# A decoder's mixtures of experts: a first tile per expert at a fixed place, gates fetched with the tokens and applied as the result leaves PSUM, outputs scattered to their tokens and added by column

## What is computed

```python
_, selected = jax.lax.top_k(scores + expert_bias[None, :], K)
top_scores = jnp.take_along_axis(scores, selected, axis=1)
top_scores = top_scores / (top_scores.sum(-1, keepdims=True) + 1e-20)
shared = jax.nn.silu(x @ shared_gate_w) * (x @ shared_up_w) @ shared_down_w
comb = jnp.zeros((T, E), jnp.float32).at[jnp.arange(T)[:, None], selected].add(top_scores)
for e in range(E):
    gu = x @ experts_gate_up[e]
    g, u = jnp.split(gu, 2, axis=-1)
    routed = routed + comb[:, e:e + 1] * (jax.nn.silu(g) * u @ experts_down[e])
return (shared + routed).reshape(b, s, h)
```

## Time and profile before

| | |
|---|---|
| median of 3 runs | 3533.64 us (3531.35 to 3537.07) |
| profiled execution, own time | 3534.41 us |
| its span, first to last instruction | 3532.6 us |
| TensorE busy | 3000.9 us (85%) |
| VectorE, ScalarE, GpSimd busy | 1560.5, 1036.7, 469.2 us |
| mean granted TensorE clock | 0.914 of full speed |
| moved by DMA | 319.04 MB, mean 90 GB/s |

### The profile page before, as it was taken

How to read it: one execution, slowest core, us unless ns; L and a number is a source line. 1 busy time by engine, 2 the same in 40 slices (tenths; PEclk the granted TensorE clock), 3 DMA queues, 4 the chain that set the end, 5 groups by cost and what they waited for, 6 DMA issues and landing times.

```text
span 3532.6 us, 36213 instructions
## 1 busy us (share of the span) xinstructions
PE 3000.9 (85%) x14276; PEld 1880.4 (53%) x14276; DVE 1560.5 (44%) x2609; ACT 1036.7 (29%) x2982; POOL 469.2 (13%) x494
## 2 busy tenths in 40 slices
PE   7889989998889999789598989999787877999951
PEld 4445454554655565467354555555444455777740
DVE  5510277103835555410365656566365667000026
ACT  3210161101723333212172223223135441444420
POOL 0000000000000000022201212120010001555555
PEclk9889989999899999899798999999798867999985
DMA  3011102100011110179300010011000002999964
GB/s 149 17 44 42 60 15 70 43 29 1 17 36 45 43 47 30 48 283 326 95 24 11 31 45 32 19 39 36 24 18 22 1 1 77 368 361 366 364 216 116
DMA packets 78377, 319.04 MB, mean 90 GB/s; under 512 B 13408, under 2 KB 13408, under 8 KB 66432
## 3 DMA queue, kind: packets, MB, share of 16 engines
q0 software_dynamic: 39264, 186.30, 15.0%
q1 hardware_dynamic: 16880, 90.19, 7.2%
q10 hardware_dynamic: 22064, 40.25, 3.1%
HBM read 274.80 MB, written 41.88 MB: 90 GB/s over the span
## 4 chain that ended last, share of the span: by engine, by line
PE 71%; DVE 17%; ACT 7%; issue 3%; POOL 2%; DMA 1%; POOLq 0%; ACTq 0%; SPq 0%; DVEq 0%
PE P L878 32%; PE P L880 14%; PE P L1199 9%; PE P L1097 3%; PE P L1079 3%; ACT A L1314 3%; PE P L886 3%; DVE A L1475 2%; PE P L891 2%; DVE A L1916 1%; POOL A L2000 1%; DVE A L1727 1%; DVE A L1725 1%; DVE A L1726 1%; ACT A L1431 1%
## 5 line engine op out<-in xcount | busy, mean ns | idle before, releaser
L878 PE MATMUL P<-A,W 128*128 128x400 f32 (+1 forms) x1888 | 691.4, 506 | 10.3 <-DVE A L1755 6.8
L1246 ACT ACTIVATE A<-P 128x400 f32<-128x400 f32 (+5 forms) x770 | 411.8, 543 | 969.1 <-PE P L880 452.3
L878 PEld LDWEIGHTS P<-A,W 128*128 128x128 f32 x1888 | 362.5, 195 | 283.9 <-issue 33.7
L2000 POOL DMA_INDIRECT A<-experts,A x141 | 134.3, 952 | 2010.2 <-DVE A L1901 1855.3
L886 PE MATMUL P<-C,A 128*128 128x128 f32 (+4 forms) x1553 | 230.4, 273 | 163.1 <-DVE A L1925 130.6
L878 PE MATMUL P<-X,W 128*128 128x400 f32 x864 | 336.6, 528 | 34.4 <-DVE X L1579 30.1
L1199 PEld LDWEIGHTS P<-A 128*128 128x128 f32 x2704 | 328.6, 194 | 69.2 <-issue 41.0
L1199 PE MATMUL P<-A 128*128 128x128 f32 x2704 | 329.6, 277 | 1.4 <-ACT A L1246 1.4
L886 PEld LDWEIGHTS P<-C,A 128*128 128x128 f32 (+4 forms) x1553 | 181.8, 149 | 206.1 <-DVE A L1925 140.1
L1916 DVE TENSOR_TENSOR A<-P,A 128x128 f32<-128x128 f32 (+1 forms) x141 | 44.9, 318 | 552.9 <-ACT A L1431 552.9
L878 PEld LDWEIGHTS P<-X,W 128*128 128x128 f32 x864 | 170.1, 201 | 165.6 <-DVE X L1579 34.1
(11 more groups left out here) (230 smaller groups left out, 3746.1 us busy)
## 6 DMA issues: line engine op xcount, KB each, us to landing
W<-weights SPq DMA_DIRECT2D x60, 1024.0 KB, 4.8
slot_outputs<-A ACTq DMA_DIRECT2D x141, 256.0 KB
W<-weights SPq DMA_DIRECT2D x32, 448.0 KB, 3.4
x_by_token<-A ACTq DMA_DIRECT2D x16, 200.0 KB
A<-experts,A POOLq DMA_INDIRECT x141
A<-x_by_token,A POOLq DMA_INDIRECT x141
W<-weights SPq DMA_DIRECT2D x8, 256.0 KB, 2.6
C<-constants SPq DMA_DIRECT2D x1, 1990.5 KB, 17.2
```

The lines of the kernel that those rows point to most:

```text
L878: self.e.matmul(out, a, b, start=i == 0, stop=False)
L1246: self.e.activation(out, in_, ACT.Copy).then_inc(*self.of(*item))
L2000: self.e.indirect_dma_start(out, None, table, bass.IndirectOffsetOnAxis(ap=idx, axis=0)).then_inc(sem, 16)
```

## The change

Places of tokens. Each expert now owns one tile of its own (`NT` = experts + `NO`), and what it has beyond 128 tokens goes into `NO` further tiles (12 and 49); the totals stay 28 and 113. Since an own tile's expert is known when the program is built, its weights are loaded by plain DMAs from SyncE (`experts`); only the further tiles' weights are fetched by an indirect DMA. `c.seq` is the order of tiles: some own tiles, then own and further ones in turn, own ones at the end. Indirect DMAs carry a bound, and rows whose index lies beyond it (empty slots, unused tiles) are not moved. Weights have 3 places in sublayer 5 and 9 in sublayer 11, of which seven are outside the old ones (dead key buffers, ring slots).

Gates. The 16 or 64 gates of a token are stored behind its 512 features (`gates_out`), come with the token rows, are picked by VectorE (`gate`), and ScalarE applies them as the scale of the copy out of PSUM. The result goes by an indirect scatter (`give`, GpSimd) to row token*kk+j of `outputs`.

Pipeline. `stages` is now fetch, two idle, xturn, up, one idle, down, give: at step t, give of tile t-7, down of t-6, up of t-4, turn of t-3, fetch of t, in both sublayers.

Adding up. `collect` is gone. SyncE loads the results of choice j for four batches at once (`YJ`, 100x4x512), two for each j, from the last j down, and VectorE adds them whole (`column`): 4 in sublayer 5, 16 in sublayer 11. In sublayer 11 the first 10 stand between the last steps of the pipeline.

Lists. `lists` is cut into `ranks`, `places`, `by_token`, `listed` and `indices`, laced with the shared expert's steps; `shared_down` comes behind them all. One of the two one-hot matrices is made by GpSimd (`place_hot`), the other by VectorE (`tile_hot`). The loops that picked gates per choice are gone. The output is stored in two halves.

```diff
-GATHERS, STORES = 16, 4
+GATHERS, STORES = 10, 9
...
-        c.NT = (T * kk + 127 * E) // 128
+        c.NO = (T * kk - kk) // 128
+        c.NT = E + c.NO
...
+        stored = [("x_stored", n, b) for b in range(NB)]
+        if n == 5:
+            c.YJ = [self.ar(3072 + 2048 * i, 4, 512) for i in range(2)]
+            c.R = 3
+            c.places = lambda: [(self.ar(12096, 3072), stored), (self.ar(21280, 3072), [("proj", "sdown", n, NB - 1)]),
+                                (self.ar(0, 3072), [("choice", n, "gates")])]
+        else:
+            c.YJ = [self.ar(2048 * i, 4, 512) for i in range(3)]
+            c.R = 9
+            idle = [("x", 7, 1)]
+            c.places = lambda: [(self.KF[:, 0:1536], idle), (self.KT[:, 0:1536], idle), (self.KT[:, 1536:3072], idle)] + [
+                (self.ring[:, SLOT * (i % RING):SLOT * (i % RING) + 1536], [self.loads[i].free]) for i in self.before(pre, "up")] + [
+                (self.ar(12096, 1536), stored), (self.ar(13632, 1536), stored)]
+        R = c.R
+        c.seq, o = [], 0
+        for e in range(E):
+            c.seq.append((c.NO + e, e))
+            while o < c.NO and e < E - kk and (o + 1) * (E - kk - R) <= (e + 1 - R) * c.NO:
+                c.seq.append((o, None))
+                o += 1
+        assert o == c.NO and all(e is not None for _, e in c.seq[:R]) and all(e is not None for _, e in c.seq[-kk:])
...
-        for f in range(c.nf):
-            for h in range(2):
-                yield "shared", c, f, h
+        both = [(f, h) for f in range(c.nf) for h in range(2)]
+        yield "ranks", c
+        for f, h in both[:2]:
+            yield "shared", c, f, h
+        yield "places", c
+        yield "shared_glu", c, 0, 0
+        yield "by_token", c
+        yield "shared_glu", c, 0, 1
+        for f, h in both[2:]:
+            yield "shared", c, f, h
+        yield "weigh_choice", c
+        for f, h in both[2:]:
+            yield "shared_glu", c, f, h
+        yield "gates_out", c
+        yield "listed", c
+        yield "indices", c
         for b in range(NB):
             yield "shared_down", c, b
-        yield "lists", c
-        idle = 2 if c.nf == 1 else 0
-        stages = ["fetch"] + [None] * idle + ["xturn", "up", "down"]
+        stages = ["fetch", None, None, "xturn", "up", None, "down", "give"]
+        columns = [("column", c, u) for u in range(2 * c.kk)]
+        landed = c.NT - c.kk + len(stages) + 1 + (c.n == 11)
         for t in range(c.NT + len(stages) - 1):
             for i in range(len(stages) - 1, -1, -1):
                 if stages[i] and 0 <= t - i < c.NT:
                     yield stages[i], c, t - i
-        first = [("norm_add", c, 0), ("norm_centre", c, 0), ("norm_scale", c, 0)]
+            if t >= landed:
+                yield columns.pop(0)
+                yield columns.pop(0)
+        yield from columns
+        first, tail = ([s for s in steps if s] for steps in self.norms(c))
         for b in range(NB):
-            for j in range(c.kk):
-                yield "collect", c, b, j
             yield "combine", c, b
             if b in (3, 4, 5):
                 yield first.pop(0)
-        return [("norm_add", c, 1), ("norm_centre", c, 1), ("norm_scale", c, 1)]
+        return tail
...
     def down(self, c, i):
         self.wait_ge(self.at("proj", "edown", c.n, i))
-        if i >= 3:
-            self.wait_ge(self.at("y_stored", c.n, i - 3))
-        self.copy(c.Y[:, i % 3, :], self.ps("proj", "edown", c.n, i)[:, :], "y", c.n, i)
-        self.wait_ge(self.at("y", c.n, i))
-        self.store(c.YD[128 * i:128 * i + 128, :], c.Y[:, i % 3, :], "y_stored", c.n, i)
+        ny = c.Y.shape[1]
+        if i >= ny:
+            self.wait_ge(self.at("given", c.n, i - ny))
+        self.wait_ge(self.at("gate", c.n, i))
+        self.e.activation(c.Y[:, i % ny, :], self.ps("proj", "edown", c.n, i)[:, :], ACT.Copy,
+                          scale=c.GW[:, i % 8:i % 8 + 1]).then_inc(*self.of("y", c.n, i))
 
...
+    def listed(self, c):
+        n, kk, NT = c.n, c.kk, c.NT
+        mark, after = self.marks(c)
+        after("tile_f")
+        for i in range(NB * kk):
+            b, j = i // kk, i % kk
+            if i >= 6:
+                self.wait_ge(self.at("plan", "list", n, i - 6))
+            self.e.tensor_scalar(c.OA[0:S, i % 6, 0:NT], self.c["tiles"][0:S, 0:NT], c.FT[0:S, b, j:j + 1],
+                                 c.DV[0:S, b, j:j + 1], ALU.is_equal, ALU.mult).then_inc(*self.of("tile_hot", n, i))
...
+    def column(self, c, u):
+
+        h = u % 2
+        a = c.ACC[0:S, 4 * h:4 * h + 4, :]
+        for part in range(2):
+            self.wait_ge(self.at("got_y", c.n, u, part))
+        if u < 2:
+            for b in range(4 * h, 4 * h + 4):
+                self.wait_ge(self.at("acc", c.n, b, -1))
+        else:
+            self.wait_ge(self.at("col", c.n, u - 2))
+        self.e.tensor_tensor(a, a, c.YJ[u % len(c.YJ)][0:S], ALU.add).then_inc(*self.of("col", c.n, u))
 
     def combine(self, c, b):
         self.wait_ge(self.at("turn", "acc", c.n, b))
...
+    def listed(self, c):
+
+        self.wait_ge(self.at("place_f", c.n))
+        for b in range(NB):
+            if b >= 4:
+                self.wait_ge(self.at("plan", "list", c.n, c.kk * (b - 3) - 1))
+            for j in range(c.kk):
+                i = self.e.tensor_scalar(c.OB[0:S, b % 4, j, :], self.c["slots"][0:S, :], c.FP[0:S, b, j:j + 1], None, ALU.is_equal)
+            i.then_inc(*self.of("place_hot", c.n, b))
+
     def fetch(self, c, i):
-        n = c.n
+        n, (d, expert) = c.n, c.seq[i]
         if i == 0:
             self.wait_ge(self.at("rows", n))
-            self.wait_ge(self.at("token_of", n))
+            self.wait_ge(self.at("indices", n))
+            self.wait_ge(self.at("empty_x", n))
             for b in range(NB):
                 self.wait_ge(self.at("x_stored", n, b))
-        if i == c.late:
-            self.wait_ge(self.at("listing", n, ("gate", c.kk - 1)))
-        if i >= len(c.WT):
-            self.wait_ge(self.at("proj", "edown", n, i - len(c.WT)))
-        self.gather(c.WT[i % len(c.WT)], c.table, c.WI[:, i:i + 1], "got_w", n, i)
-        if i == 0:
-            self.wait_ge(self.at("proj", "sdown", n, NB - 1))
-            self.wait_ge(self.at("acc", n, NB - 1, -1))
+            self.wait_ge(self.at("gates_stored", n))
+        if expert is None:
+            self.wait_ge(self.at("proj", "edown", n, i - c.R))
+            self.rows(c.places()[i % c.R][0], None, c.table, c.WI[:, d:d + 1], 128 * c.E - 1, "got_w", n, i)
         if i >= 4:
             self.wait_ge(self.at("turn", "x", n, i - 4))
-        self.gather(c.XG[:, i % 4, :], self.k.XD[:, :], c.TI[:, i:i + 1], "got_x", n, i)
-
-    def collect(self, c, b, j):
-        m = b * c.kk + j
-        if m == 0:
-            for i in range(c.NT - STORES, c.NT):
-                self.wait_ge(self.at("y_stored", c.n, i))
-            self.wait_ge(self.at("proj", "edown", c.n, c.NT - 1))
-        if m >= 8:
-            self.wait_ge(self.at("acc", c.n, (m - 8) // c.kk, (m - 8) % c.kk))
-        self.gather(c.YG[0:S, m % 8, :], c.YD[:, :], c.SI[0:S, b, j:j + 1], "got_y", c.n, m)
+            self.wait_ge(self.at("gate", n, i - 4))
+        self.rows(c.XG[:, i % 4, :], None, c.XD[:, :], c.TI[:, d:d + 1], T - 1, "got_x", n, i)
+
+    def give(self, c, i):
+        d = c.seq[i][0]
+        self.wait_ge(self.at("y", c.n, i))
+        self.rows(c.YD[:, :], c.YI[:, d:d + 1], c.Y[:, i % c.Y.shape[1], :], None, T * c.kk - 1, "given", c.n, i)
...
+    def experts(self, c):
+
+
+        R = c.R
+        for i, (d, expert) in enumerate(c.seq):
+            if expert is None:
+                continue
+            place, needs = c.places()[i % R]
+            for item in needs if i < R else [("proj", "edown", c.n, i - R)]:
+                self.wait_ge(self.at(*item))
+            self.dma(f"expert{i % R}", place, c.table[128 * expert:128 * expert + 128, :], "got_w", c.n, i)
+        by_column = c.YD.rearrange("(b s j) n -> j s b n", b=NB, j=c.kk)
+        given = 0
+        for u in range(2 * c.kk):
+            j, h = c.kk - 1 - u // 2, u % 2
+            for i in range(given, c.NT - j):
+                self.wait_ge(self.at("given", c.n, i))
+            given = c.NT - j
+            if u >= len(c.YJ):
+                self.wait_ge(self.at("col", c.n, u - len(c.YJ)))
+            for part, rows in enumerate((slice(0, 96), slice(96, S))):
+                self.dma(f"given{u % 3}_{part}", c.YJ[u % len(c.YJ)][rows], by_column[j, rows, 4 * h:4 * h + 4, :], "got_y", c.n, u, part)
...
+            if p.index >= RING and k.loads[p.index - RING].name == ("L2_attn_", "qk", 1):
+                self.experts(k.subs[5])
+            self.piece(p, wd)
+        self.experts(k.subs[11])
```

More of the change, by code:

```diff
@@ L1853, in lists, with places @@
+    def places(self, c):
+        E, n, sm = c.E, c.n, self.k.small
+        mark, after = self.marks(c)
```

(11 more changed lines are left out.)

273 lines of the change are left out of this document (157 added, 116 removed).

## The result

The changed kernel takes 3498.05 us (median of 4 runs, 3491.65 to 3499.11) against 3532.67 (4 runs, 3531.35 to 3537.07): a ratio of 0.9895, 95% interval 0.9883 to 0.9908. It is faster by 1%. The prediction said 3429 and 3398 to 3466: right in direction, but 69 us too low, and the measured time lies above the range. The profiled execution is the quickest of the four, with an own time of 3491.65 and a span of 3489.8.

A forecast was written before the change was run, and what follows sets the result against it. TensorE and its hand-offs were taken to pace sublayer 11's loop, DMA only just keeping up. 3532.6 - 23 - 31 - 56 + 5 (sublayer 5) = 3427.6 us span, forecast 3429 us, 8-in-10 range 3398 to 3466.

The forecast's parts named there:

- skipped rows cost like moved ones: Rival for both tile loops: unmoved rows cost full DMA time, +37 and +13 us, giving 3479; chance 7%.
- GpSimd sets the loop: Rival for sublayer 11's loop: indirect DMAs at 1.454 us make GpSimd set the pace, +27 us, giving 3456; chance 14%.
- the clock in sublayer 5: Rival: each stall lowers TensorE's clock for a tile, 1.5 to 2 us nine times, giving 3445; chance 10%.
- Sublayer 11's start, -23 forecast: Sublayer 11 before its tile loop: one-hots shared by two engines, gate loops gone, first `down` at 2975 against 2998.
- end at 2960.5: Sublayer 11's lists: one-hots start at 2940 and end at 2960.5, GpSimd taking 0.3 us each; 0.45 would add 9.
- The rival of one-hots in turns: Sublayer 11's lists: VectorE and GpSimd block each other, their one-hot times add up, +10 us, giving 3439; chance 12%.
- Sublayer 5's loop, +27 forecast: Sublayer 5's tile loop: three weight places cause stalls costing +45 us, shorter steps of 5.83 us give back 18.
- a wait of under 1 us that the following stall swallows: Sublayer 5's loop: own tiles' weights land in 6.0 plus 0.5 us against steps of 5.83, at no net cost.
- Sublayer 5's start, -9 forecast: Sublayer 5 before its loop: expert loads wait for `shared_down`, ending 1495.5; first `down` at 1516 against 1525.5.
- The ends, -56 and -12 forecast: Behind the last `down`: column loads and adds replace gathers, 71.4 against 127.6 us in sublayer 11, 35.7 against 48.1 in 5.
- loads of 800 KB land in 4.25 us: Column loads at the ends: with three places and 2.33 us of adding, 2.3 us a column, just hidden.
- Sublayer 11's loop, -31 forecast: Sublayer 11's tile loop: 112 steps of 3.36 us, 376 against 407; at 3.18, hand-off fully hidden, -51.

The follow-up runs named there:

- e1: Changed kernel with both one-hot matrices of the lists made by VectorE, none by GpSimd: 3571.0 us, sublayer 11's start 79.6 us.
- e5: Changed kernel with four places of weights in sublayer 5 instead of three, long pipeline kept: 3425.1 us, ratio 0.9691 to the kernel before.
- f1: Changed kernel with VectorE one-hots, four weight places in sublayer 5, its first own weights queued ahead of the dense pieces, columns read in one stretch: 3401.6 us.
- f2 to f4: Three single edits of the changed kernel: most adding left out; columns read in one unbroken stretch; expert weights read instead of results. 3490.0, 3492.7, 3498.0 us.
- g2: Changed kernel with result columns in unbroken 800 KB stretches, each loaded into 128 partitions of 1600 elements instead of 96 and 4 of 2048: 3474.1 us.
- h1: Changed kernel with unbroken result columns, loads writing only partitions 0 to 63 and almost no adding: 3566.7 us, sublayer 11's end 73.2 us.
- h2: Changed kernel with unbroken result columns, loads writing only partitions 32 to 95 and almost no adding: 3540.0 us, sublayer 11's end 61.9 us.
- f2: Changed kernel with VectorE adding only 8 of 512 features of each column, loads, places and waits as they were: 3490.0 us.
- c1_after_again: The changed kernel itself run once more, unedited, on a second chip: 3494.5 us, ratio 0.9888 to the kernel before.

## Why the prediction failed

Of the 69 us, 62 are in the profiled execution, and the stages below add up to them; the rest is that the median lies 6.4 us above that execution, where the sum had it 0.8 under. Five stages missed by 8 to 19 us each, and one came out 9 us better. The two rivals nearest to 3498, 3479 (skipped rows cost like moved ones) and 3456 (GpSimd sets the loop), are near by luck: in sublayer 11's loop the DMA share is 0.60 and TensorE has no wait in the step shown. What did come of the rivals is the clock in sublayer 5.

**Sublayer 11's start, -23 forecast, -4.0 measured.** The step that failed is "end at 2960.5: GpSimd is the slower hand, and I give it 0.3 us each, as VectorE's 0.29", with a price of 0.45 as the worse case. GpSimd takes 0.59 to 0.69 each, 64 of them 40.0 us where 20.5 were counted. The one-hots did begin where the sum had them, even 7 us sooner (29.7 us behind the router's second half, which is 2933 in before's trace). Another 6.4 us lie between the last one-hot and the first `down`: 4.3 until `shared_down` starts, since TensorE can work off the last batch of eight pairs only then, and 9.9 us for `shared_down` in one row where 7.7 were counted. A price taken from another engine's row is no bound.

The 20.5 us were out of reach for another reason too, which stands in the rows: TensorE needs 3.76 us for eight pairs, 0.43 from one to the next. That is an estimate of 27 to 28 us for 64 however fast the one-hots are made; e1's list takes 28.75, and sublayer 11's start is then 79.6 where the sum had 71.6. So of the 19 us that were missed about 11 are GpSimd's, by e1, and 8 remain without it.

The rival of one-hots in turns does not come. The Trainium skill (SBUF: State Buffer, "SBUF: two separate sides") has one of the two engines block fully where VectorE is in a two-port mode or reads two SBUF inputs; which mode the one-hots ran in no row shows. In this trace six of VectorE's pass in 1.79 us within GpSimd's unbroken row, and GpSimd's own take 0.59 or 0.60 to 0.62, at most 0.03 us more. No turns are seen.

**Sublayer 5's loop, +27 forecast, +43.8 measured.** The mechanism of the stall was right, and its sum, 45 against a measured 35.7 + 10.1 = 45.8, is in part luck. For the tokens the sum had 4.8 nine times and 2 for the rest; the waits for tokens are 35.7, seven of 3.38 to 5.40 us and four short ones. The 10.1 are waits of `up` for own tiles' weights, loaded by SyncE, which the sum put at nothing ("a wait of under 1 us that the following stall swallows"); they are 0.2 to 1.9 us each, twelve times. What the sum left out is "the clock falls in sublayer 5", which stood among the rivals with 10%, at 1.5 to 2 us for each of nine stalls. Without stalls (e5) 27 steps take 151.0, 24 less than before where the sum had 18 less; 151.0 + 45.8 leaves 22 of the 218.9. They are TensorE's: the same 1044 matmuls are busy 173.1 us in the changed kernel and 150.6 in e5, where the clock is 1.00. e5 takes away only the stall, and the slow matmuls go with it. Half-clock rows follow seven stalls, so it is about 3 us each, not 2.

**Sublayer 5's start, -9 forecast, +3.6 measured.** The mechanism was right, weights behind pieces that wait for `shared_down`, and the lists were ready about when the sum had them (first token rows at 1492.74, forecast about 1490). The step that failed is the end of `shared_down`, "1495.5 by the same count as above": in this sublayer it has 32 matmuls, twice as many as in the other, starts at 1490.84 behind the lists and takes 15.6 us, to 1506.4. GpSimd's one-hots have no part in it, since e1 leaves the stage as it is. f1 shows what the queue order is worth, 11 us.

**The ends, -56 and -12 forecast, -38.9 and -4.4 measured.** The step "loads of 800 KB land in 4.25 us" failed: they land in 8.0. It was read from loads of 1024 and 448 KB into all 128 partitions; these write partitions 0 to 95 and 96 to 99. In sublayer 11 the last column ends 50.6 us behind the last `down`'s start, against 32.4; what follows takes 38.1 against 39. f2 to f4 exclude the adding, the order of reading and the source; g2 and h1 to h2 leave which partitions are written. Of 100 partitions 64 lie in the lower half, 0 to 63, where an even split would put 50; 0 to 63 alone passed at 207 GB/s, 32 to 95 at 305. The Trainium skill (SBUF: State Buffer, "Door 1: The DMA port swizzle") states that partitions 0 to 63 reach 8 of 16 ports and 0 to 127 all; this case's 207 against 305 and 299 GB/s agree. By its table the 100 rows put 8 partitions on each port of the lower half, as many as 128 rows do, so they would take as long as the 1,048,576 bytes of 128 such rows. At g2's 299 GB/s that is an estimate of 3.5 us a column; 3.61 was measured. The prediction could have had it from that page.

In sublayer 5 the missing 7.6 us are less clear. The first column starts 11.0 us behind the last `down`, and only two places serve four columns. Sublayer 5's end takes 38.3 with 128 partitions (g2) in place of 43.6, but 34.6 and 34.0 in h1 and h2, so there the choice of partitions makes 0.6; leaving out the adding (f2) gives 3.7. How the three share it is not shown.

```profile
1758.12 2.29 DVE L2044 TENSOR_TENSOR A<-A 100x2048 f32<-100x2048 f32 x1 [11.69 <-DMA A<-outputs]
```

**Sublayer 11's loop, -31 forecast, -40.4 measured.** The bound was right and the choice wrong: the hand-off is hidden wholly, 3.18 a step, the lower value of the two. 112 steps of 3.18 are 356. Of the other 10 us, 8.8 are waits for tokens, ten of them, and 2.5 a wait of the last `down` for VectorE, where its product stands behind a column of 2.29 us. GpSimd keeps up: 77 of 100 us busy, at 1.02 to 1.03 us an indirect DMA rather than 0.94.

## What to carry to other kernels

When stages are inserted between a buffer's last reader and its writer, count the places again: one place of weights too few cost 68 us, more than the change as a whole gained. An operation moved to another engine has no price until that engine has a row of it; the same holds for a DMA that writes other partitions. Before one engine's share of a hand-off is made shorter, read from the rows how fast the engine behind it can go. A stall on TensorE is to be counted with the slow matmuls behind it, here 22 us on top of 46.

## What the runs showed of the hardware

- A 100x128 one-hot costs GpSimd 0.59 us (changed kernel, beside an idle VectorE), VectorE 0.28 (e1).
- A load's rate hangs on which partitions it writes. In the windows of the tails: partitions 0 to 63 207 GB/s, 32 to 95 305, all 128 299, 0 to 95 and 96 to 99 217, each with the DMA engines 0.87 to 0.97 busy; 100 rows in one DMA 203 at 0.66. Columns laid out so that both halves of the partitions take as much were not tried.
- On two of five chips sublayer 11's loop takes 442 to 462 us in place of 365 to 369, in all six variants that ran there, with standstills of ScalarE and GpSimd of up to 5 us whose releaser the trace doesn't know. Before's times are the same on all five (3532.7 to 3535.4), though its loop has the higher DMA share, 1.00. What stops the engines is open, and so is whether f1_best keeps its lead there: neither it nor c1_after_again ran there. Chip and hour were not separated.
